# First cross-attention: the row maxima handed over head by head instead of in pairs

## The reference

```python
qh = _split_heads(q @ Wq + bq, B)
kh = _split_heads(k @ Wk + bk, B)
vh = _split_heads(v @ Wv + bv, B)
logits = jnp.einsum('bhqd,bhkd->bhqk', qh, kh) / jnp.sqrt(jnp.asarray(PROJ_DIM, jnp.float32))
tril = jnp.tril(jnp.ones((S, S), dtype=logits.dtype))
logits = logits + jnp.log(tril * 1e-09 + 1e-09)
attn = jax.nn.softmax(logits, axis=-1)
out = jnp.einsum('bhqk,bhkd->bhqd', attn, vh)
```

## Time and profile before

| what | us |
|---|---|
| three timed runs, median (lowest to highest) | 1750.9 (1742.44 to 1754.22) |
| the profiled execution | 1747.78 |
| its span, first to last instruction | 1745.9 |
| PE busy in the span | 1583.2 (91%) |
| DVE busy | 1238.0 (71%) |
| ACT busy | 1000.5 (57%) |
| POOL busy | 773.9 (44%) |
| the reduction of the maxima, line 1525, 128 times | 156.7 |

### The profile page before, as it was taken

The page is one execution under the profiler, slowest core; times in us unless marked ns, Lnnn a source line. Parts: engine busy times, 40 slices in busy tenths (PEclk is TensorE's granted clock), DMA queues, the critical chain, the costliest instruction groups (busy, mean ns, idle before and its releaser), DMA issues. The chain is left out here.

```text
span 1745.9 us, 45012 instructions
## 1 busy us (share of the span) xinstructions
PE 1583.2 (91%) x16664; PEld 1222.3 (70%) x16664; DVE 1238.0 (71%) x3676; ACT 1000.5 (57%) x1742; POOL 773.9 (44%) x948
## 2 busy tenths in 40 slices
PE   4699999879899999999999789998888689999997
PEld 3456666458788888888888445666554479898874
DVE  5888888857556655656677679988987266757768
ACT  5578877665445444544433455675654358777752
POOL 4256657787401000001165434332464153677765
PEclk9899999989999999999999889999998799999999
DMA  6556556242365545455453454332344356899954
GB/s 191 136 124 137 119 107 142 53 110 89 90 206 182 194 133 194 133 168 184 140 167 121 93 86 86 65 70 54 74 87 124 151 173 221 260 298 292 315 174 145
DMA packets 297740, 257.03 MB, mean 147 GB/s; under 512 B 198079, under 2 KB 270187, under 8 KB 296248
## 3 DMA queue, kind: packets, MB, share of 16 engines
q1 hardware_dynamic: 271288, 168.84, 36.0%
q0 software_dynamic: 26240, 85.32, 15.0%
HBM read 102.98 MB, written 107.74 MB: 121 GB/s over the span
## 5 line engine op out<-in xcount | busy, mean ns | idle before, releaser
L1868 PE MATMUL ps<-m_xT,m_w_halves 128*128 128x256 f16 x3360 | 413.4, 273 | 0.0
L1868 PEld LDWEIGHTS ps<-m_xT,m_w_halves 128*128 128x128 f16 x3360 | 329.1, 98 | 38.8 <-ACT a_probs L1299 0.4
L1299 ACT ACTIVATE a_probs<-ps 128x1024 f32<-128x1024 f32 (+1 forms) x256 | 234.7, 917 | 165.6 <-PE ps L1111 163.7
L1899 PE MATMUL ps<-m_w_halves,m_hiddenT 128*128 128x256 f16 x1680 | 231.2, 274 | 8.8 <-DVE m_hiddenT L2027 5.8
L1953 ACT ACTIVATE m_hiddenT<-m_hidden 128x256 f16<-128x256 f32 x280 | 116.5, 416 | 213.4 <-DVE m_hidden L2022 213.4
L1426 POOL TENSOR_TENSOR a_probs<-a_probs,a_half_above 128x512 f32<-128x512 f32 x128 | 163.8, 1281 | 131.4 <-ACT a_probs L1299 131.0
L2027 DVE TENSOR_TENSOR m_hiddenT<-m_hidden,m_hiddenT 128x256 f16<-128x256 f32 x280 | 119.3, 426 | 124.5 <-ACT m_hiddenT L1953 124.1
L1823 POOL DMA_DIRECT2D expert_out<-m_y x40 | 29.0, 725 | 382.2 <-DVE m_y L2010 189.3
L1111 PE MATMUL ps<-a_Q,a_K 32*128 32x256 f16 (+1 forms) x2048 | 155.2, 265 | 36.6 <-DVE a_qT L1525 24.4
L1525 DVE TENSOR_REDUCE a_qT<-ps 128x4 f16<-128x1024 f32 x128 | 156.7, 1224 | 44.4 <-PE ps L1120 43.5
L1899 PEld LDWEIGHTS ps<-m_w_halves,m_hiddenT 128*128 128x128 f16 x1680 | 163.7, 98 | 33.1 <-DVE m_hiddenT L2027 10.9
(11 more groups left out here) (314 smaller groups left out, 3071.1 us busy)
## 6 DMA issues: line engine op xcount, KB each, us to landing
routed<-m_zeros POOLq DMA_DIRECT2D x32, 768.0 KB, 3.9
r_space<-routed SPq DMA_DIRECT2D x48, 512.0 KB, 5.3
routed_out<-m_y SPq DMA_DIRECT2D x48, 512.0 KB
r_w_load<-in_L_w SPq DMA_DIRECT2D x24, 896.0 KB, 7.2
dispatched<-r_x_halves SPq DMA_DIRECT2D x10, 1024.0 KB, 5.4
expert_out<-m_y POOLq DMA_DIRECT2D x40, 256.0 KB, 2.6
a_ctx_in<-in_ctx SPq DMA_DIRECT2D x32, 256.0 KB, 2.9
m_experts_load<-in_L_experts SPq DMA_DIRECT2D x18, 384.0 KB, 3.6
```

The source lines that it names most:

```text
L1299: A(pr[:, g % 2, 2 * jp:2 * jp + 2, :], SC[:, :, 0:SPAN], ACT.Exp, scale=1.0 / math.sqrt(DH)).then_inc(asem["ex"], 1)
L1868: last = mm(psum[:, v % HB, m * CH:(m + 1) * CH], wh[u][:, ws_, m, d_ * F0 + f_ * P:d_ * F0 + (f_ + 1) * P], xT[:, q % XB, xs_ * KT + d_, ...
L1899: last = mm(down_of(q, t), hT[:, hs_, f_, t * P:(t + 1) * P], wh[u][:, ws_, 2, f_ * D:(f_ + 1) * D], start=f_ == 0 and k == 0, stop=f_ == ...
```

## The change

In the first attention PE now makes the maxima products by head, as in the second. Both products of the first head follow the first part of the first scores, both of the second head the first part of the second scores. Each head has its own wait (`max0`, `max`) in front of its products and its own signal (`mx0`, `mx`) behind them. DVE takes each head's bank in a reduction of its own, 128x512 elements to 128x2, waits for each head alone and signals after each. `mx0` has a semaphore of its own, which before it shared with the mask; for that, the counter of the last stores is now a used one whose value starts at 1.

```diff
-               krot=1, qrot=1, kf=1, qf=1, qdup=1, mask=8, neg=2, max0=8)
-    rope_only = ("krot", "qrot", "kf", "qf", "neg", "max0")
-    asem = {k: sem("a_mask_then_mx0" if k == "mask" else "a_" + k) for k in PER}
-    asem["mx0"], PER["mx0"] = asem["mask"], PER["mask"]
+               krot=1, qrot=1, kf=1, qf=1, qdup=1, mask=8, neg=2, max0=8, mx0=8)
+    rope_only = ("krot", "qrot", "kf", "qf", "neg")
+    asem = {k: sem("a_" + k) for k in PER}
...
-                    if not causal_band:
-                        need_latest(pe, ("max", i + 1, s - 1) if s else ("max", i, 7))
-
...
-                def maximum(t):
-                    for b_, j in enumerate(jb):
-                        r = slice(j * SLOT, (j + 1) * SLOT)
-                        last = mm(MX[:, b_, t * S:(t + 1) * S], Q1[r, w_, g, t * P:(t + 1) * P], K1[r, w_, g, 0:S],
-                                  start=True, stop=True, tile_position=(j * SLOT, 0))
-                    if t == TT - 1:
-                        last.then_inc(asem["mx"], 1)
-
                 def maximum_of_head(b_):
                     done = "max" if b_ else "max0"
                     need_latest(pe, (done, i + 1, s - 1) if s else (done, i, 7))
                     r = slice(jb[b_] * SLOT, (jb[b_] + 1) * SLOT)
                     for t in range(TT):
-                        last = mm(MX[:, b_, t * P:(2 * t + 1) * P], Q1[r, w_, g, t * P:(t + 1) * P],
-                                  K1[r, w_, g, 0:(t + 1) * P], start=True, stop=True,
+                        cols = slice(t * P, (2 * t + 1) * P) if causal_band else slice(t * S, (t + 1) * S)
+                        last = mm(MX[:, b_, cols], Q1[r, w_, g, t * P:(t + 1) * P],
+                                  K1[r, w_, g, 0:cols.stop - cols.start], start=True, stop=True,
                                   tile_position=(jb[b_] * SLOT, 0))
                     last.then_inc(asem["mx" if b_ else "mx0"], 1)
 
                 for kt in range(TT):
                     if scoring:
                         score(kt, False)
-                    if maxing and causal_band:
+                    if maxing:
                         maximum_of_head(kt)
-                    elif maxing:
-                        maximum(kt)
                     if scoring:
                         score(kt, True)
...
-                if not causal_band:
-                    need(dve, "mx", m, s)
...
-                    last = V.tensor_reduce(qT2[:, m % 3, :, h0:h0 + 2, DH].rearrange("p t h -> p h t"),
-                                           MX.rearrange("p h (t k) -> p h t k", t=TT), AX.X, ALU.max, negate=True)
+                    for b_ in range(2):
+                        need(dve, "mx" if b_ else "mx0", m, s)
+                        last = V.tensor_reduce(qT2[:, m % 3, :, h0 + b_, DH], MX[:, b_, :].rearrange("p (t k) -> p t k", t=TT),
+                                               AX.X, ALU.max, negate=True)
+                        if b_ == 0:
+                            last.then_inc(asem["max0"], 1)
                 last.then_inc(asem["max"], 1)
...
-        stored = sem("stored")
+        stored, STORED0 = r_T, 1
...
-                sp.wait_ge(stored, 16 * (RG + 2))
+                sp.wait_ge(stored, STORED0 + 16 * (RG + 2))
```

More of the change, by code:

```diff
@@ L117, in flamingo_kernel @@
     b_T, bo_mm, bo_sum, b_hi = sem("a_bias_transposed"), sem("a_bo_product"), sem("a_bo_summed"), sem("a_bias_hi")
-    r_T = sem("a_rope_transposed")
+    r_T = sem("a_rope_transposed_then_rows_stored")
     gate_set = sem("gate_set")
```

## The result

The changed kernel is slower by a little: a median of 1753.91 us (20 runs) against 1748.34 (20 runs of the kernel before beside them), a ratio of 1.0033 with a 95% interval of 1.0020 to 1.0047. That lies within the 1% that the prediction called no change, and within its range, but on the other side of its forecast of -3.7 us. The profiled execution took 1758.96 us (span 1757.2).

The account below looks back on a forecast made before the run. PE was taken to set the pace over most of the first attention, DVE near its end. Terms of -4.1, -1.8 and +2.2 us gave -3.7, so 1747.8 became 1744.1, or 1747 on the median's scale; range 1729 to 1762.

Parts of the forecast that it names:

- PE's products by head, 0: First attention, PE: the same 512 products in another order were taken to cost 0, at the other end 28 us.
- The late handover, 0.31 us to the next work: First attention: from a late second head to PE's next work 0.31 us against 0.55, saving 0.24 us each time.
- PE's waits between half and three quarters of 29.1: First attention: sign that the forecast is right, PE's waits for the reductions coming to that share of 29.1 us.
- the waits go: Rival: PE's waits for DVE in the first attention vanish, under 10 us as sign; 1720 to 1735 us, chance 0.15.
- what is late next: First attention, after a saved wait: mostly PE's own work or exp, with score weight loads waiting 23.7 us for ScalarE.
- DVE's wait well under 43.5: First attention: sign that the forecast is right, DVE's wait for PE's products falling well below 43.5 us.
- +0.04 us a step for the reductions: First attention, DVE: two half-size reductions hold it 1.18 us against 1.14; +2.2 us over 56 reductions on the path.
- The sum of -3.7 us over 128 steps: First attention: handovers -4.1 us, direct cases -1.8 us and DVE's reductions +2.2 us, together -3.7 us.
- Semaphores ... No operation changes: 0: Counters: parting the mask's counter from mx0 and counting the last stores on a used one was to cost 0.
- costs nothing: PE's two waits inside a first-attention step: one already satisfied was to cost nothing, as seen in the second attention.
- What is gained there should reach the end: Behind the first attention PE goes on with the first experts, so the gain there should show in the whole time.
- PE's order: Rival: a head's second product holds up PE's queued scores, 0.22 us a step, 28 us; 1773 us, chance 0.06.

Follow-up runs that it names:

- e1: The kernel before with only the maxima products handed out head by head, one wait, signal and reduction kept; ratio 1.0005 to the kernel before.
- e2: The kernel before with only the one reduction split into two of 512 elements, one per bank; ratio 1.0018 to the kernel before.
- e0: The kernel before, run again unchanged against itself; ratio 0.9979, with 148.35 us between steps 24 and 84.
- f2: The kernel before with only PE's wait for the free banks moved from the step's front to the first maxima product; ratio 1.0030 to the kernel before.
- f1: The kernel before with only the edits to the semaphore counters; ratio 0.9992 to the kernel before.
- h1: The changed kernel with an always satisfied wait added at step fronts, putting PE's program back to 21353 instructions; ratio 0.9992 to the kernel before.
- f0: The changed kernel run again, unchanged; ratio 1.0017 to the kernel before.
- g1: The changed kernel run once more, unchanged, in a later round; ratio 1.0035 to the kernel before.
- h2: The kernel before with 152 more semaphore instructions at the start of PE's program, where it stands idle; ratio 1.0050 to the kernel before.
- h4: The kernel before with 128 more semaphore instructions at the start of PE's program; ratio 1.0016 to the kernel before.
- g2: The changed kernel with DVE's 128x16 sum of the scatter's row numbers moved behind the next step's reductions; ratio 1.0032 to the kernel before.

## Why the prediction was wrong, point by point

- *PE's products by head, 0:* right (e1).
- *The late handover, 0.31 us to the next work:* right, 0.32. *PE's waits between half and three quarters of 29.1:* too little, they fell to 8.2 us, below the 10 us that were to show that "the waits go"; but the wait for exp rose from 5.6 to 13.0, as "what is late next" had it, and the gain stayed small. *DVE's wait well under 43.5:* missed, 39.4.
- *+0.04 us a step for the reductions:* mis-sized, 1.20 against 1.14 is 0.06; alone (e2) it costs 0.016 us a step in the even part, since most steps hide it.
- *The sum of -3.7 us over 128 steps:* in the even part it came true against e0: -1.67 us over 60 steps, where 60/128 of 3.7 is 1.73. In part that is luck, since its terms came out otherwise: the late wait alone gains 1.58 (f2), and the two reductions alone cost 0.96 (e2), so that handing over by head would have given about 1.0 if the parts add. Outside the table's three distances single profiles of one program differ by more than such sums, and I claim nothing there.
- *"Semaphores ... No operation changes: 0", and a satisfied wait that "costs nothing":* this step failed. The counters are indeed free (f1). But a wait is also an instruction in PE's program; its place decides whether it is one of its own, and I counted signals and products, never instructions. 104 fewer moved the later loads of code, and the second attention lost 4.1 us in the changed kernel's profile; with the 104 put back (h1) it lost nothing.
- *"What is gained there should reach the end":* failed with it. In the changed kernel 2.4 us go to the collision of DVE with GpSimd at step 84 and the lower clock behind it, and 4.1 to the late gather and the lower clock in the second attention: -1.7 + 2.4 + 4.1 is +4.8 us, for 5.8 by the first ratio. The same sum is +2.1 for f0 and +4.3 for g1, for 3.0 and 6.1 by their ratios. For the late wait alone it gives +0.6 against 5 and 7 measured, and for h2 +2.1 against 8.7, so further losses must exist outside these distances. Other loads meeting other transfers, or a clock lower elsewhere, would be causes, but neither is shown.
- *The rivals:* none was it. The one that ended on the slow side, PE's order, was not there; the clock was lower (0.960 for 0.964 to 0.966), and with the code's position put back (h1) it was 0.964 again. So the lower clock comes with the shifted code, yet it costs time of its own (1.5 us at step 80); how much of the 5.8 us is the clock's is open.

## What to carry to other kernels

Count a change in instructions of each engine's program, not only in operations and waits: here 104 semaphore instructions fewer on PE moved the later code loads, and in this long straight-line program the time was lost 700 us behind the edit (128 instructions more on DVE cost nothing there). When time is lost where nothing was edited, look at the instruction queue and the granted clock there, and test the code's position by padding the program at an idle place; and run the unchanged kernel against itself, since here the same program came out at 0.9979.

## What was new about the hardware

- With a code packet 2.7 to 3.6 us behind a gather's issue, among transposing loads, DVE's wait for the gather was 2.19 to 3.11 us for 0.52 to 0.89, in eight of nine profiles; in g1 the gather's packets were through 2.8 us before DVE was released. The packet itself takes 1.4 to 1.5% of the engines' time in 4 us. Why so small a load goes with so long a wait is not shown, nor why h4 escaped.
- The same program can lose 1.6 us in one step in which the granted clock is down (0.57 for 1.00 over 4 us): 149.94 for 148.35 us between steps 24 and 84 of the kernel before.
- A 128x16 operation of VectorE with two operands took 1.24 us for 0.17 when a 1.26 us operation of GpSimd had begun 0.05 us earlier, and 0.16 again when it was moved away (g2). This is a matter of tenths of a microsecond, and a change that makes another engine faster can bring it about.
- One distance of the kernel is reproducible to a few hundredths: steps 32 to 96 of the second attention took 178.19 to 178.24 us in the nine profiles of kernels with 21353 instructions (the one ahead of the prediction among them), and 180.28 to 182.32 in the nine others. Other distances are not: the 32 steps ahead of it took 85.8 to 91.3 us in the same nine profiles. Where a distance holds still, single profiles can tell a loss of 0.2 us in a run whose whole time scatters by 15.
